# Last batch's row sums, values and output projection placed ahead of the expert groups in a one-core attention and expert kernel

## The reference, cut to what matters

```python
h = x + attention(rmsnorm(x, g1), wq, wk, wv, wo)     # 16 heads of 64, 4 key/value heads, causal
out = h + moe(rmsnorm(h, g2), router_w, router_b, w1, w2, w3)

# moe: 8 experts, top 2, capacity 256 tokens per expert over ALL 2048 tokens
logits = xf @ router_w + router_b
vals, idx = top_k(logits, 2)
scores = softmax(vals)
pos = cumsum(cumsum(one_hot(idx), axis=0), axis=1)     # over the tokens, in order
emask = one_hot * (pos < cap)
m = max(assigned expert)                                # one expert per token
y = gelu((xf @ w2[m]) * (xf @ w1[m])) @ w3[m]
slot = y where the choice was admitted, else xf
out = sum_k slot_k * scores_k
```

## Time and profile before

| | us |
|---|---|
| median of 3 runs | 603.54 (603.06 to 603.59) |
| the profiled execution, its own time | 601.87 |
| its span, first to last instruction | 600.1 |
| PE busy | 483.9 (81%) |
| DVE busy | 384.3 (64%) |
| ACT busy | 228.9 (38%) |
| POOL busy | 161.0 (27%) |
| mean granted TensorE clock | 0.941 of full speed |

### The profile page before, as it was taken

One profiled execution on the slowest core, in us unless ns is written; L12 is line 12 of the kernel. 1 busy time (PEld: TensorE's weight loads), 2 busy tenths in 40 slices (PEclk: granted clock), 3 DMA queues, 4 the chain that ended last, 5 costly groups with the idle time before them and its releaser, 6 DMA issues.

```text
span 600.1 us, 8119 instructions
## 1 busy us (share of the span) xinstructions
PE 483.9 (81%) x2788; PEld 267.8 (45%) x2788; DVE 384.3 (64%) x1104; ACT 228.9 (38%) x418; POOL 161.0 (27%) x200
## 2 busy tenths in 40 slices
PE   4766685899889979987998899799779788885930
PEld 2333352454354535544563555355355345554620
DVE  3518679657748565776668486555877426772784
ACT  1241440464283246417432742364143242343400
POOL 4210602300413230224304131303406650034531
PEclk9977997899999999999999999899989899997965
DMA  7400000000011003000300020021061341013213
GB/s 207 148 1 1 1 1 2 2 1 1 3 34 40 1 4 73 1 3 1 72 2 3 3 69 2 3 49 25 2 187 40 104 93 52 10 54 92 63 52 88
DMA packets 19094, 23.82 MB, mean 40 GB/s; under 512 B 2630, under 2 KB 15374, under 8 KB 18158
## 3 DMA queue, kind: packets, MB, share of 16 engines
q1 hardware_dynamic: 15308, 18.19, 11.2%
q0 software_dynamic: 1648, 4.07, 2.5%
q10 hardware_dynamic: 2098, 1.05, 0.6%
HBM read 16.71 MB, written 6.28 MB: 38 GB/s over the span
## 4 chain that ended last, share of the span: by engine, by line
PE 53%; DVE 18%; ACT 10%; issue 9%; DMA 5%; POOL 4%; ACTq 1%; POOLq 0%; DVEq 0%; SPq 0%
PE ps_r L923 6%; ACT pt L1686 6%; PE ps_st L888 5%; PE ps_r L711 4%; PE ps_r L797 4%; PE ps_r L658 4%; PE ps_r L950 4%; DVE rmax L1187 3%; DVE rmax_a L1187 3%; PE ps_st L877 3%; PE ps_r L939 3%; PE ps_r L781 3%; POOL qkr L551 2%; PE ps_st L1087 2%; DMA oT<-inv_dram 2%
## 5 line engine op out<-in xcount | busy, mean ns | idle before, releaser
L551 POOL TENSOR_TENSOR qkr<-qkr,prod 128x512 f32<-128x512 f32 (+1 forms) x48 | 52.2, 1093 | 208.7 <-DVE prod L1303 207.6
L1187 DVE TENSOR_REDUCE rmax_a<-ps_r 128x2 f32<-128x512 f32 (+1 forms) x96 | 61.7, 685 | 26.2 <-PE ps_r L781 25.6
L658 PE MATMUL ps_r<-cbt 128*128 128x256 bf16 (+1 forms) x192 | 63.0, 328 | 5.0 <-DVE rmax_a L1187 2.4
L1187 DVE TENSOR_REDUCE rmax<-ps_r 128x2 f32<-128x512 f32 (+1 forms) x96 | 61.5, 683 | 4.8 <-PE ps_r L902 4.5
L588 POOL TENSOR_TENSOR oT<-pvb,oT 128x1024 f32<-128x1024 f32 x14 | 32.8, 2364 | 108.0 <-DMA oT<-inv_dram 108.0
L1695 ACT ACTIVATE pt<-ps_st 128x1024 f32<-128x1024 f32 x48 | 47.2, 1022 | 36.1 <-PE ps_st L888 36.1
L923 PE MATMUL ps_r<-pt,vb 128*64 128x512 f32 x192 | 48.9, 617 | 4.9 <-ACT pt L1695 3.2
L1686 ACT ACTIVATE pt<-ps_st 128x1024 f32<-128x1024 f32 x48 | 46.5, 1022 | 13.4 <-PE ps_st L696 13.1
L950 PE MATMUL ps_r<-wqkv,xT_b 128*128 128x512 f32 x96 | 47.2, 631 | 3.2 <-DVE rmax_a L1187 3.2
L781 PE MATMUL ps_r<-kq_a 128*128 128x512 f32 x96 | 46.6, 544 | 0.0
L1315 DVE TENSOR_TENSOR qbuf<-ps_r,qbuf 128x512 fp32r<-128x512 f32 x32 | 20.7, 686 | 34.3 <-ACT qbuf L1770 34.3
(11 more groups left out here) (238 smaller groups left out, 910.7 us busy)
## 6 DMA issues: line engine op xcount, KB each, us to landing
oT<-inv_dram SPq DMA_DIRECT2D x14, 512.0 KB, 6.3
xs_dram<-pvb SPq DMA_DIRECT2D x1, 2048.0 KB
pt<-in_L_ffn_w SPq DMA_DIRECT2D x2, 1024.0 KB, 7.7
ys_dram<-qkr SPq DMA_DIRECT2D x14, 128.0 KB, 1.8
qkr<-xs_dram POOLq DMA_DIRECT2D x4, 256.0 KB, 3.8
x_all<-in_L_attn_x ACTq DMA_DIRECT2D x1, 896.0 KB, 6.7
pvb<-xs_dram POOLq DMA_DIRECT2D x3, 256.0 KB, 3.6
out<-x_all SPq DMA_DIRECT2D x1, 640.0 KB, 3.8
```

Of the source, the lines that this page charges most:

```text
L551: nc.gpsimd.tensor_tensor(part, part, prod[:, (3 * t + i) % 2, 0:w], ALU.add).then_inc(add_in, 1)
L658: nc.tensor.matmul(o[:, :, P * (i >= 4):], ident_b, qmask.unsqueeze(1).broadcast_to([P, heads, P]), start=True, stop=False, skip_group_che ...
L1187: nc.vector.tensor_reduce(heads_of(i), ps_r[:, b, :].rearrange("p (h k) -> p h k", h=4 if i < 4 else 2), AX.X, ALU.max).then_inc(free[b], 1)
```

## The change

The edit does five things. (1) `divide_values` writes to a new buffer `oT_last`, made of three quarters in `wqkv` (the projection weights, which nobody reads any more then) and one in `pvs`; so it needs no wait for `bo1`, and has a semaphore of its own, `last_in`. Its first half moves up behind `invert_weights(7, 0)`. (2) In step 7 PE does the slots of group 0, the row sums ws10 and ws11 and the values bv3 first, and then both projections in a row, batch 6's and batch 7's. (3) DVE does the second half of the sums and division, then batch 6's residual and norm, then batch 7's residual and norm, before the first group; batch 7's root now comes from ACT's Ln and Exp with one correction step, where it was nine small DVE instructions. (4) ACT does both roots after it has taken bv3, ahead of the load of Gelu's table. (5) The routing pieces stand at earlier groups: logits of batch 6 at (0, 1) where (1, 0) was, `xfT` and logits of batch 7 at (1, 0) and (1, 1) where (2, 0) and (3, 0) were, `cnt1` at (2, 1) where (4, 0) was, `rk1` at (3, 1) where (5, 0) was; DVE's pieces go with them.

```diff
-           NB - 1: {"sm0": [(NB - 1, "ws00"), (NB - 1, "ws01")], "bv3": [], "xfT": [], "lg": [],
-                    "sm1": [(NB, "xg0"), (NB - 1, "ws10"), (NB - 1, "ws11"), (NB - 1, "bv3")]}}
-BETWEEN = {(0, 0): [(NB - 1, "xfT")], (0, 1): [(NB, "bo0"), (NB, "bo1")], (1, 0): [(NB - 1, "lg")],
-           (2, 0): [(NB, "xfT")], (3, 0): [(NB, "lg")], (4, 0): [(NB, "cnt1")], (5, 0): [(NB, "rk1")]}
+           NB - 1: {"sm0": [(NB - 1, "ws00"), (NB - 1, "ws01")], "bv3": [], "bo0": [], "bo1": [], "xfT": [], "lg": [],
+                    "sm1": [(NB, "xg0"), (NB - 1, "ws10"), (NB - 1, "ws11"), (NB - 1, "bv3"),
+                            (NB - 1, "bo0"), (NB - 1, "bo1"), (NB, "bo0"), (NB, "bo1")]}}
+BETWEEN = {(0, 0): [(NB - 1, "xfT")], (0, 1): [(NB - 1, "lg")], (1, 0): [(NB, "xfT")], (1, 1): [(NB, "lg")],
+           (2, 1): [(NB, "cnt1")], (3, 1): [(NB, "rk1")]}
...
+        flat_w = wqkv[:, :]
+        oT_last = [[x.rearrange("p (g c) -> p g c", g=G) for x in y]
+                   for y in ((flat_w[:, 0:512], flat_w[:, 512:1024]), (flat_w[:, 1024:1536], pvs[:, 1, :]))]
...
             def divide_values(s, t):
-                if t == 0:
-                    filled(dve, s, "bo1")
                 emptied(dve, s, ("bv1", "bv3")[t])
                 for k in range(HKV // 2):
-                    ins = TT(oT[:, k, t], pvb[s % 2][:, k, t, :].rearrange("p (g c) -> p g c", g=G),
+                    ins = TT(oT_last[k][t], pvb[s % 2][:, k, t, :].rearrange("p (g c) -> p g c", g=G),
...
-                    ins.then_inc(oT_in, 1)
+                    ins.then_inc(last_in, 1)
...
# PE, step 7
-                if "TB" in on:
+                if "TB" in on and s < NB - 1:
                     project_out(s)
...
                     weights(s, 1)
                     values(s, 3)
+                    project_out(s)
+                    project_out(NB)
...
# DVE, ahead of the groups
-            divide_values(NB - 1, 1)
+            dve.wait_ge(xf_in, NB - 1)
+            residual(NB, NB - 1)
+            mean_square(y, root_t, chain_t, CHAIN_B * (NB - 1), var_t)
+            dve.wait_ge(r0_t, NB)
+            newton(root_t, chain_t, CHAIN_B * (NB - 1) + 2)
+            dve.wait_ge(xfa_in, NB - 1)
+            filled(dve, NB - 1, "xfT")
+            for t in range(NT):
+                ins = V.scalar_tensor_tensor(xf[:, t, :], y[:, t, :], root_t.r[:, t:t + 1], g2b[:, :], ALU.mult, ALU.mult)
+            ins.then_inc(xf_in, 1)
...
# ACT, step 7
                 take_values(s, 3)
+                if s == NB - 1:
+                    inverse_root(root_t, var_t, ln_t, r0_t, NB - 1)
+                    inverse_root(root_t, var_t, ln_t, r0_t, NB)
```

More of the change, by code:

```diff
@@ L395, in build @@
         inv_in = sem("inv_in")
-        oT_in = sem("oT_in")
+        oT_in, last_in = sem("oT_in"), sem("last_in")
         chain_a, chain_p, chain_t = sem("chain_a"), sem("chain_p"), sem("chain_t")
@@ L793, in project_out @@
                     o = fill(s, f"bo{t}")
-                    if t == 0:
+                    if t == 0 and s < NB:
                         pe.wait_ge(oT_in, 1 + s)
+                    if t == 0 and s == NB:
+                        pe.wait_ge(last_in, 1)
                     for j in range(H // 2):
-                        mm = nc.tensor.matmul(o[:, 0:C], oT[:, j % 2, t, j // 2, :], wob[:, j, :],
+                        of = oT[:, j % 2, t, j // 2, :] if s < NB else oT_last[j % 2][t][:, j // 2, :]
+                        mm = nc.tensor.matmul(o[:, 0:C], of, wob[:, j, :],
                                               start=j == 0, stop=j == H // 2 - 1)
@@ L1117, in between @@
                         ranks(1)
-                    if name == "bo0":
-                        project_out(at)
                     if name == "xfT":
@@ L1345, in step @@
                     invert_weights(s, 0)
+                    divide_values(s, 0)
                 maxima_a(s, 2, 4)
@@ L1367, in step @@
                 maxima_a(s, 6, 8)
+                if s == NB - 1:
+                    invert_weights(s, 1)
+                    divide_values(s, 1)
                 if "TB" in on:
@@ L1392, in step @@
                     split(s, 0)
-                if s == NB - 1:
-                    divide_values(s, 0)
-                    invert_weights(s, 1)
                 if "TB" in on and s < NB - 1:
@@ L1617, in between @@
                 if (n, half) == (0, 1):
-                    residual(NB, NB - 1)
-                    mean_square(y, root_t, chain_t, CHAIN_B * (NB - 1), var_t)
-                if (n, half) == (1, 0):
                     take_logits(NB - 1, NB - 2)
-                    dve.wait_ge(var_t, NB)
-                    newton_root(root_t.v[:, :], root_t.a[:, :], root_t.r[:, :])
-                    dve.wait_ge(xfa_in, NB - 1)
-                    for t in range(NT):
-                        ins = V.scalar_tensor_tensor(xf[:, t, :], y[:, t, :], root_t.r[:, t:t + 1], g2b[:, :],
-                                                     ALU.mult, ALU.mult)
-                    ins.then_inc(xf_in, 1)
-                if (n, half) == (3, 0):
+                if (n, half) == (1, 1):
                     take_logits(NB, NB - 1)
                     first_choices(1)
-                if (n, half) == (4, 0):
+                if (n, half) == (2, 1):
                     admit(1)
-                if (n, half) == (5, 0):
+                if (n, half) == (3, 1):
                     slots(1)
@@ L1875, in _ @@
                 copy(n, g)
-                if n == 0:
-                    turned_tokens(NB - 1)
+                if n < 2:
+                    turned_tokens(NB - 1 + n)
                 if n + 1 < NG:
@@ L1880, in _ @@
                 gelu(n, g)
-                if n == 1:
-                    turned_tokens(NB)
                 if n == 7:
```

## The result

The changed kernel took 597.3 us (median of 16 runs, 594.55 to 601.45), the kernel before 602.83 us in the same comparison (16 runs, 601.03 to 605.17): a ratio of 0.9904, with a 95% interval of 0.9884 to 0.9923. That is 5.5 us less, where 7.0 were forecast.

What follows compares the result with a forecast made beforehand. The end was taken to be set by when `sidx` is written, through scatters and reload to xg9. Routing 7.0 us earlier, with nothing gained or lost behind it, took 603.54 to 596.5 us; range 594.0 to 599.3.

Steps and rivals of the forecast that it cites:

- The reading of step 7: PE's reordered sums, values and projections: about 1 us wait for the exponentials, up(0) at 505.8, 4.2 us later.
- the new wait behind the table load: PE behind up(0), ahead of batch 6's logits: idle 2 us for ACT, whose Gelu table load takes 1.3 us.
- The rival by which the change does nothing: Something other than `sidx` releases the first scatter, so the hole only changes sides: 603.5 us, chance 0.04.
- The slower rival: Clock falls behind up(0) and stays at 1.2 GHz up to xg9: 619 us at most, chance 0.03.
- A reading of the page: The page's slices: PE busy falls to five and four tenths between 540 and 570 us.
- the hole ends a fixed distance behind the routing: From `sidx` written to xg9, 14.72 us of DMAs and POOL alone, carried over unchanged.
- I leave the 1.6 us in: From xg9 to up(10): a 2.7 us hole still brings the clock down, costing 1.6 us as before.
- the clock stays up at the hole: Rival at PE's hole ahead of xg9: no clock fall, 1.6 us won as well, 594.9 us, chance 0.16.
- Nothing behind it: Behind xg9, scatter, reload, pass 1's groups, gathers and last norm keep their distances: no further gain or loss.
- The tables at group 7: ACT's two table loads, 2.8 us, no longer covered by the hole, end near 539.0: just hidden before up(9) at 540.8.
- 1.97 us no fall, 2.03 fall: PE waits in the old profile: clock kept up after idling 1.97 us, at 1.2 GHz after 2.03 us.
- The rival that the clock falls behind up(0): At PE's new 2 us wait ahead of the logits, 1.6 us lost on the chain: 598.1 us, chance 0.12.

Runs made afterwards that it cites:

- free scatters: Changed kernel with pass 1's six scatters issued without waiting for the one two places ahead to land: 594.34 us, ratio 0.9868.
- the second comparison: The second four of twelve follow-up kernels, on one chip with its own runs of the kernel before: median 603.3 us (18 runs).
- The two kernels with filled holes: Extra matmuls on constants ahead of xg9's wait: 14 in the changed kernel, 596.97 us; 27 in the kernel before, 601.31 us.
- three filled holes: Changed kernel with 14 extra matmuls ahead of xg9 and eight more ahead of each of two further waits: 595.55 us, ratio 0.9875.
- free gathers: Changed kernel with pass 1's scatters and pass 0's ten gathers all issued without waiting for landings: 609.94 us, ratio 1.0014.

## Why the prediction was right, and where it was off

**Everything up to the scatter was right to 0.3 us.** up(0) was forecast at 505.8 and stood at 505.74, up(1) 510.7 and 510.72, `sidx` 524.9 and 525.15, the first scatter 525.8 and 525.99, PE through at 537.0 and 537.32. The reading of step 7 held, including its idle time (0.97 us for the exponentials) and the new wait behind the table load (2 us, 2.17). PE's only other waits up to the hole are 0.18 us for ACT's `xfT` behind up(1) and 0.48 at group 5, behind DVE's pieces, where 0.5 in all was allowed.

**The cause was right.** The kernel with the routing late took away all of the gain, the one with it one group later about half. The rival by which the change does nothing is out. The profile of the changed kernel still puts the first scatter's wait down to issue, but with free scatters it names `sidx`, and the scatter follows it by 0.8 to 0.9 us in all profiles:

```profile
527.01 1.08 POOL L564 DMA_INDIRECT xs_dram<-x_all,sidx  x1 [21.03 <-DVE sidx L1530]
```

The slower rival is out too: in the two profiles in which the clock fell at the wait of 2.17 us behind up(0) it was back at 1.00 from 516 on.

**A reading of the page that was wrong.** PE is down to five tenths between 540 and 555 us only; from 555 to 570 it is at nine, and the next low slice, three tenths, begins at 570. No term of the sum stood on this.

**Mis-sized: from `sidx` to xg9.** I carried over 14.72 us as a fixed distance. It was 16.03, and 1.3 us of the 6.8 stayed there: the hole was 3.85 us, not 2.7. The step that failed is "the hole ends a fixed distance behind the routing". The distance holds waits for scatters to land, and these differ from profile to profile. It was 14.1 to 16.0 us in the ten profiles with that limit on scatters, 15.1 to 16.0 in the four of them with the changed kernel's routing, and 13.28 with free scatters in the second comparison.

**Mis-sized: the clock.** I put 1.6 us for the fall, from 5.79 less an undisturbed 4.2. The two kernels with filled holes show 4.87 as the undisturbed distance; it holds a pause of 0.43 us behind up(9) that the 4.2 had left out. So the fall had cost 0.9 us, not 1.6, and now costs 1.9 instead of the same. The stretches of the kernel before, columns as above, show how:

```profile
542.00:544.00 2.00, 0.00 (x0) 0.78 0.10 33
544.00:546.00 2.00, 0.00 (x0) 0.50 0.59 147
...
548.00:550.00 2.00, 2.00 (x7) 0.51 0.01 2
```

There the clock fell at about 543.1 and was back at about 550; half of that was idle time ahead of xg9. In the changed kernel it fell at 539.6, for about as long, and work started at 541.2. The hole that became shorter left more of the low stretch to the work behind it. That was another 1.0 us given back, on "I leave the 1.6 us in".

The rival "the clock stays up at the hole" did not happen in either profile of the changed kernel, but it was no far one: behind a hole of 2.64 us, the size that was forecast, the clock stayed up in the kernel with more table loads.

**"Nothing behind it" was nearly so.** 0.9 us more went between up(10) and the last product. The forecast put this at nothing: it let the gathers keep their distance. The one wait that has grown there is DVE's for the last gather of pass 0, and the chain of waits runs through it (the gather, then DVE):

```profile
567.82 2.73 DMA pt<-ys_dram,gidx
```
```profile
570.64 1.40 DVE L1600 SCALAR_TENSOR_TENSOR x_all<-pt,kz,x_all 128x128 f32<-128x128 f32 x5 [0.89 <-DMA pt<-ys_dram,gidx]
```

From up(10) to the last product it is 24.9 us in the kernel before, without such a wait, and 25.8 here. The other profiles of the first two comparisons line up: five without the wait have 24.9 to 25.1, with more table loads it is 25.3 and a wait of 0.31, with three filled holes 25.8 and 0.86, and with the routing one group later 26.6 and 1.72:

```profile
572.13 1.40 DVE L1600 SCALAR_TENSOR_TENSOR x_all<-pt,kz,x_all 128x128 f32<-128x128 f32 x5 [1.72 <-DMA pt<-ys_dram,gidx]
```

So the last product is late by about the length of this wait. No kernel took the wait away alone: the one with free gathers had the pauses.

**The tables at group 7** were through in time, as forecast: the loads stand at 536.52 and 538.04, and from xg9 to up(9) it is 2.18 us, as before (2.19).

**The reading "1.97 us no fall, 2.03 fall" was wrong.** A wait near 2 us gives a fall in some executions and not in others. The rival that the clock falls behind up(0) was therefore no case of its own with 598.1, but something that happens in part of the runs: in two profiles of seven with this wait. It cost 1.2 and 1.7 us at `sidx`; that it makes a part of the 1% by which runs of one kernel differ is likely, not shown.

In sum: of 6.8 us at `sidx`, 1.3 went at the scatters, 1.0 at the clock, 0.9 up to the last product and 0.3 behind it, and the profile shows 3.3 at the last DVE instruction. The medians show 5.5, so if `sidx` moves as far in a usual run, only about 1.3 of these 3.5 us of losses are there, and which of them isn't known. A profile is one execution; the difference of two of them was off by 2.3 us here, more than any of the four. That 5.5 came near 7.0 bears out where the chain starts, not the single terms behind it.

## What to carry to other kernels

When the end is set by a chain of DMAs, ask when that chain starts, not how busy the engines are: here the whole gain came from moving a few small operations by one to two groups, and the work that was reordered for it showed no gain alone. Don't carry a DMA stretch over as a fixed distance if it holds waits for landings; take the range that it shows elsewhere in the trace. A wait on PE of 2 us or more may be paid a second time by the clock, and a shorter hole need not make that second payment smaller: it was largest here behind holes of 3.8 us. And a chain that starts earlier can meet the next limit: here the gathers.

## What the runs showed of the hardware

**A table load took 1.28 us and nothing else**: 1.29 from start to start, three in a row, with the next instruction right behind.

**DVE and POOL slow each other down.** The first half of the division now can run beside POOL's product, and where it did both took longer. DVE's and POOL's rows:

```profile
486.12 3.44 DVE L1434 TENSOR_TENSOR wqkv<-pvb,smb 128x512 f32<-128x512 f32 x2
```
```profile
486.17 5.63 POOL L592 TENSOR_TENSOR oT<-pvb,oT 128x1024 f32<-128x1024 f32 x2 [7.93 <-DMA oT<-inv_dram]
```

Two such multiplications took DVE 1.29 us where nothing ran on POOL, here 3.44, 0.69 for the first and 2.84 for the second; POOL's product took 4.68 in the kernel before, here 5.63. In the kernel with the routing one group later DVE was through before POOL began, and they took 1.29 and 4.68 again. The Trainium skill (SBUF — State Buffer, Who interferes with whom) states that a DVE instruction with two inputs from SBUF contends with a GpSimd instruction that reads SBUF, and calls that an exclusive lock. The trace agrees: DVE's second multiplication, begun at 486.7, ended 0.6 us behind POOL's first half (486.17 to 489.0), and from the first start to the last end it is 5.7 us, near the sum of 1.29 and 4.68. It cost no time here, since PE wanted the product at 498.49 only.

**The clock's fall is not a matter of the wait alone**: with the same program and the same wait of 2.17 us it fell to 1.2 GHz in one execution and stayed at 2.4 in another, and it stayed at 2.4 over a wait of 2.64 us in a third kernel. What decides it was not found.
